# Tensor product of a graph network: rows of the bracket product numbered weight row first

## What is computed

```python
w = _mlp(emb, fc1_w1, fc1_w2)            # relu(emb @ w1) @ w2, per edge: 4 blocks of 16 x 8
s_t = a1 * (einsum('eu,euw->ew', s1, Wss) + einsum('eu,euw->ew', vdot1, Wvv))
v_t = a1 * (einsum('eu,euw->ew', s1, Wsv)[:, :, None] * sh1[:, None, :] + einsum('euk,euw->ewk', v1, Wvs))
w2 = _mlp(emb, fc2_w1, fc2_w2)           # 6 blocks of 8 x 8, used in the same way on s_t and v_t
edge_out = concatenate([tanh(scal), (vecs * tanh(gates)[:, :, None]).reshape(E, 24)], axis=1) * norm[:, None]
return segment_sum(edge_out, edge_dst, num_segments=num_nodes)
```

## Time and profile before

| | us |
|---|---|
| median of three runs | 27219.49 (27213.19 to 27268.23) |
| the profiled execution, span from first to last instruction | 31250.7 |
| of it the tensor product's stretch, 21460 to 31214 | 9754 |
| busy over the span: PE, DVE, POOL, ACT | 15884.3, 15483.3, 15773.3, 5202.4 |

### The profile page before, as it was taken

How to read it: one execution, slowest core, us unless ns; L and a number is a source line. 1 busy time by engine, 2 the same in 40 slices (tenths; PEclk the granted TensorE clock), 3 DMA queues, 4 the chain that set the end, 5 groups by cost and what they waited for, 6 DMA issues and landing times. The chain is left out here.

```text
span 31250.7 us, 456719 instructions
## 1 busy us (share of the span) xinstructions
PE 15884.3 (51%) x102440; PEld 9300.4 (30%) x102441; DVE 15483.3 (50%) x31596; ACT 5202.4 (17%) x13760; POOL 15773.3 (50%) x16798
## 2 busy tenths in 40 slices
PE   7344444445555558973000000035777777777776
PEld 5233333333333338861000000022222222222222
DVE  9444444445555554442111115975555555555556
ACT  4111111111111114431000000001222222222222
POOL 0355555556666664442666666722444444444444
PEclk9555555555555555555555555556777777777777
DMA  2444444432222224521223222212444444444443
GB/s 65 100 121 120 120 120 121 119 91 58 58 59 59 58 56 146 154 81 31 82 81 80 80 80 75 72 47 72 92 93 91 92 92 90 93 91 92 92 92 90
DMA packets 2854618, 2738.27 MB, mean 88 GB/s; under 512 B 1309983, under 2 KB 2216029, under 8 KB 2851618
## 3 DMA queue, kind: packets, MB, share of 16 engines
q1 hardware_dynamic: 2287198, 2308.39, 28.2%
q0 software_dynamic: 412544, 241.53, 5.5%
q10 hardware_dynamic: 153668, 172.93, 2.1%
HBM read 2173.27 MB, written 537.90 MB: 87 GB/s over the span
## 5 line engine op out<-in xcount | busy, mean ns | idle before, releaser
L2219 POOL DMA_INDIRECT rows_x<-x_table,index x3125 | 2973.0, 951 | 4269.0 <-DMA index<-in_src 3504.1
L742 POOL DMA_INDIRECT rows<-split_table,index x3125 | 2985.2, 955 | 3665.8 <-DMA index<-in_src 2695.3
L858 POOL DMA_INDIRECT rows<-x_table,index x3125 | 3296.4, 1055 | 1720.6 <-issue 914.5
L1624 POOL DMA_INDIRECT rows_dram<-rows,place_now x3125 | 3025.4, 968 | 2130.5 <-DVE rows L1552 1145.9
L2333 DVE TENSOR_TENSOR second<-banks,h 128x768 f32<-128x768 f32 x2500 | 1949.2, 820 | 1731.5 <-PE banks L2488 1520.0
L1564 PE MATMUL banks<-row_pieces,hot_turned 128*128 x3125 | 390.1, 289 | 4176.5 <-issue 2856.4
L2325 DVE TENSOR_TENSOR first<-banks,h 128x768 f32<-128x768 f32 x2500 | 1969.4, 820 | 1043.5 <-DMA rows_dram<-rows,place_now 399.2
L1552 DVE TENSOR_REDUCE rows<-banks 128x108 f32<-128x324 f32 x1250 | 490.6, 434 | 4022.9 <-issue 2683.7
L550 PE MATMUL banks<-counts,low_turned 128*128 128x98 f32 x6250 | 1810.5, 438 | 427.2 <-ACT counts L538 318.2
L550 PEld LDWEIGHTS banks<-counts,low_turned 128*128 128x128 f32 x6250 | 1614.6, 317 | 556.0 <-issue 525.0
L2463 PE MATMUL banks<-u_turned,w_tensor 32*128 32x384 f32 (+1 forms) x10000 | 1614.3, 545 | 262.5 <-DVE second L2333 206.0
(11 more groups left out here) (479 smaller groups left out, 34278.3 us busy)
## 6 DMA issues: line engine op xcount, KB each, us to landing
key_row<-dst_rows SPq DMA_DIRECT2D x1250, 320.0 KB
h<-hidden_dram SPq DMA_DIRECT2D x1250, 320.0 KB
acc_moved<-dst_rows SPq DMA_DIRECT2D x625, 320.0 KB
src_row<-in_src_rows SPq DMA_DIRECT2D x625, 320.0 KB
hot_turned<-turned_dram SPq DMA_DIRECT2D x1250, 160.0 KB
hot_dram<-onehot SPq DMA_DIRECT2D x625, 160.0 KB
turned_dram<-hot_turned SPq DMA_DIRECT2D x625, 160.0 KB
a_dram<-a ACTq DMA_DIRECT2D x625, 160.0 KB
```

Source lines behind the costliest of these rows:

```text
L742: nc.gpsimd.indirect_dma_start(out=m["rows"][j][:, t * SPLIT:(t + 1) * SPLIT], out_offset=None, in_=m["split_table"], in_offset=bass.Indir ...
L858: nc.gpsimd.indirect_dma_start(out=m["rows"][j][:, t * C2:t * C2 + F], out_offset=None, in_=m["x_table"], in_offset=bass.IndirectOffsetOnA ...
L1624: nc.gpsimd.indirect_dma_start(out=m["rows_dram"], out_offset=bass.IndirectOffsetOnAxis(ap=m["place_now"][j][:, t:t + 1], axis=0), in_=m[" ...
L2219: nc.gpsimd.indirect_dma_start(out=m["rows_x"][j][:, t * F:(t + 1) * F], out_offset=None, in_=m["x_table"], in_offset=bass.IndirectOffsetO ...
```

## The change

A bracket's row is numbered (k, u), the hidden row first, instead of (u, k). So an `h` tile is loaded with the 16 rows outermost and each repeated eight times. The tables must follow: `w_tensor` is loaded in the old order into a new tile `w_loaded` and permuted by one DVE copy; `w_second`'s 48 small loads go to a new DRAM tensor `second_dram`, from which two loads bring it back in the new order, after a wait for all 48; `unit_sum` and `unit_spread` compare the row number modulo 8 instead of divided by 16.

```diff
@@ stage_directions, SP
-            w, v = m["w_tensor"], m["conv_w1"]
+            w, v = m["w_loaded"], m["conv_w1"]
...
-                    rows = m["w_second"][K16 * u:K16 * (u + 1), 4 * U8 * dotted:4 * U8 * (dotted + 1)]
+                    rows = m["second_dram"][:, u, 4 * U8 * dotted:4 * U8 * (dotted + 1)]
...
-                        sp.dma_start(rows[:, k * U8:(k + 1) * U8], part, allow_slow_non_contiguous=True).then_inc(s["weights"], 16)
+                        sp.dma_start(rows[:, k * U8:(k + 1) * U8], part, allow_slow_non_contiguous=True).then_inc(s["placed"], 16)
...
+            sp.wait_ge(s["placed"], 16 * 6 * U8)
+            for dotted in range(2):
+                here = slice(4 * U8 * dotted, 4 * U8 * dotted + 3 * U8)
+                sp.dma_start(m["w_second"][:, here], m["second_dram"].rearrange("k u c -> (k u) c")[:, here]).then_inc(s["weights"], 16)
@@ stage_directions, DVE
-            for name in ("w_tensor", "w_second"):
+            for name in ("w_loaded", "w_second"):
...
-            dve.wait_ge(s["weights"], 16 * (8 + 6 * U8))
+            dve.wait_ge(s["weights"], 16 * (8 + 2))
+            link(nc.vector.tensor_copy(m["w_tensor"][:, :].rearrange("p (c k u) -> p c k u", k=K16, u=U8),
+                                       m["w_loaded"][:, :].rearrange("p (c u k) -> p c k u", k=K16, u=U8)))
...
-            link(nc.vector.tensor_single_scalar(m["unit_int"][:, :], m["unit_int"][:, :], 4, ALU.arith_shift_right))
+            link(nc.vector.tensor_single_scalar(m["unit_int"][:, :], m["unit_int"][:, :], U8 - 1, ALU.bitwise_and))
@@ sp_group
-                         m["hidden_dram"][bass.ds(g, 1), K16 * k:K16 * (k + 1), :].rearrange("g h e -> (g h) e").unsqueeze(0).broadcast_to([U8, K16, T * P])
+                         m["hidden_dram"][bass.ds(g, 1), K16 * k:K16 * (k + 1), :].rearrange("g h e -> (g h) e").unsqueeze(1).broadcast_to([K16, U8, T * P])
```

More of the change, by code:

```diff
@@ L43 @@
 ONE, FULL = 1, 16
-FROM_ZERO = ("loaded", "x_loaded", "attr_in", "stored", "indexed", "row_in", "pair_in", "a1_in", "emb_in", "weights", "step",
+FROM_ZERO = ("loaded", "x_loaded", "attr_in", "stored", "indexed", "row_in", "pair_in", "a1_in", "emb_in", "weights", "placed", "step",
              "gathered", "moved", "hidden_in", "axes_in", "halves_in", "weights_in", "src_row_in", "marked", "scattered", "own_in", "vec_in", "place_in", "key_in", "key_out", "repeated", "blank_out", "hot_in", "turned_in")
@@ L2058, in _ @@
                 for u in range(U8):
-                    rows = m["w_second"][K16 * u:K16 * (u + 1), 4 * U8 * dotted:4 * U8 * (dotted + 1)]
+                    rows = m["second_dram"][:, u, 4 * U8 * dotted:4 * U8 * (dotted + 1)]
                     for k in range(2):
                         part = m["conv_w2"][:, (1 - k) * P:(2 - k) * P].rearrange("k (o e n) -> k o e n", e=2, n=U8)[:, :, dotted, u]
-                        sp.dma_start(rows[:, k * U8:(k + 1) * U8], part, allow_slow_non_contiguous=True).then_inc(s["weights"], 16)
+                        sp.dma_start(rows[:, k * U8:(k + 1) * U8], part, allow_slow_non_contiguous=True).then_inc(s["placed"], 16)
                     part = m["conv_w2"][:, 256 + 64 * dotted:320 + 64 * dotted].rearrange("k (o n) -> k o n", n=U8)[:, :, u]
-                    sp.dma_start(rows[:, 2 * U8:3 * U8], part, allow_slow_non_contiguous=True).then_inc(s["weights"], 16)
+                    sp.dma_start(rows[:, 2 * U8:3 * U8], part, allow_slow_non_contiguous=True).then_inc(s["placed"], 16)
+            sp.wait_ge(s["placed"], 16 * 6 * U8)
+            for dotted in range(2):
+                here = slice(4 * U8 * dotted, 4 * U8 * dotted + 3 * U8)
+                sp.dma_start(m["w_second"][:, here], m["second_dram"].rearrange("k u c -> (k u) c")[:, here]).then_inc(s["weights"], 16)
             sp.wait_ge(s["permuted"], ONE + 2)
@@ L2720, in build @@
         m["dirs_dram"] = nc.dram_tensor("dirs_dram", (P, COLS * 3), F32, kind="Internal").ap()
+        m["second_dram"] = nc.dram_tensor("second_dram", (K16, U8, 8 * U8), F32, kind="Internal").ap()
         m["dst_rows"] = nc.dram_tensor("dst_rows", (COLS, P), F32, kind="Internal").ap()
@@ L2919, in build @@
                 sb("squared", max(COLS * 3, HALF_WINDOWS * F), into=inner); sb("length", COLS, into=inner)
-                sb("unit_int", P + 1, I32, into=inner); sb("unit", P + 1, into=inner)
-                stage_directions(nc, m, sems("dirs", "halves_in aimed loaded weights stored step cleared permuted to_root rooted"))
+                sb("unit_int", P + 1, I32, into=inner); sb("unit", P + 1, into=inner); sb("w_loaded", 512, into=inner)
+                stage_directions(nc, m, sems("dirs", "halves_in aimed loaded placed weights stored step cleared permuted to_root rooted"))
             with ExitStack() as inner:
```

## The result

The change takes 26539.97 us (median of four runs, 26524.74 to 26628.84) against 27216.34 for the kernel before, run beside it (27169.51 to 27268.23): ratio 0.9764 [0.9749, 0.978], 676 us less. The forecast was 26630, with a range of 26000 to 26930.

What follows compares the result with a forecast made beforehand. The index list, landing behind h in SP's queue, was taken to bound a two-turn loop. 205 x 3.3 = 677 us, less 5 for setup, is 672, scaled to 585 off 27219.49: 26630 us, range 26000 to 26930.

Steps and rivals of the forecast that it cites:

- The engines (8 to 16): Tensor product's h load: with 16 instead of 8 outermost it runs on sixteen DMA engines instead of eight.
- The price of a loop, 3.3 us: Tensor product's two-turn loop: the index list lands earlier, 3.3 us off each loop, bounds 2.0 and 4.8.
- The part from the burst: Transfer of h and hot_half ahead of the list: 6.0 us falls to 4.0 to 2.6, so 2.0 to 3.4 off.
- The part from SP's issue: SP's h issue falls from 621 ns to key_row's 333, so the index list is issued 0.6 us earlier.
- The count, 205 loops: Tensor product: 205 of 312 loops run through the index list, from its 1288 us of the chain.
- The scale, 0.871: The 672 us gain on the profiled span of 31250.7 is scaled by 0.871 to the runs' median: 585 us.
- The setup, 5 us: Stage before the tensor product: w_second's way through DRAM and the new DVE copy cost 5 us, far end 14.
- A mark that was set wrong: Profile after, tensor product: POOL's wait for lists at 4.50 - 3.3 = 1.2 us a turn or little more.
- The split stays: Rival: h's engines don't follow the outer size, so only the setup moves: 27224 us; chance 0.06.
- All loops gain, holes too: Rival: the chain's unnamed holes shrink too, all 312 loops lose up to 4.8 us: 25910; chance 0.17.
- Another wait: Rival: another wait takes the list's place and half the gain is given back: 26925 us; chance 0.10.
- Slower: Rival: one engine reading the same DRAM row eight times running is slow, the burst grows: 27655 us; chance 0.05.

Runs made afterwards that it cites:

- b_early: The kernel before, with each group's index list loaded one group earlier: 25164.38 us, ratio 0.9236.
- a_early: The change, with each group's index list loaded one group earlier: 25160.2 us, ratio 0.9235.
- two_by_rows: The change, with each h load cut into two issues by rows, 8 outermost: 27059.52 us, ratio 0.9945.
- eight_by_cols: The kernel before, with each h load cut into two issues of half the columns, 8 outermost: 27022.91 us, ratio 0.9931.
- two_by_cols: The change, with each h load cut into two issues of half the columns, 16 outermost: 26531.83 us, ratio 0.9754.
- distinct: The change, with each h load reading 128 different rows in plain form from the sixth group on (results not the program's): 26187.4 us, ratio 0.9629.
- one_row: The change, with each h load reading a single DRAM row into all 128 partitions (results not the program's): 26646.1 us, ratio 0.9797.

## Why the prediction was right, and where it was off

**Right: what bounds, and why.** The list behind h on SP's queue, reached from DVE's release and passed on by POOL to PE, is the loop; `b_early` and `a_early` show that the change gains nothing without it. The engines (8 to 16) are what moved it: `two_by_rows` and `eight_by_cols` against `two_by_cols`, and the list's late parts, eight before and none after. Sign and range held.

**The price of a loop, 3.3 us, measured 2.5** (11.34 to 8.82; 2.35 by the chain's pieces). The part from the burst is 2.44 (7.39 to 4.95), inside the 2.0 to 3.4. The part from SP's issue failed: 0.6 was expected because key_row, as many rows of the same size, issues in 333 ns. But 550 ns is what 16 x 8 x 640 takes; only the plain forms of `distinct` and `one_row` come to 333. It gave 0.08 of the list's time.

**The count, 205 loops, was too small.** It came from the shown execution's chain, where the list had 13.2% and unnamed holes over a third; counted, that chain has 191 pieces of the list. The execution that matches the runs has 290, and PE's 295 waits for pieces say the same. 289 x 2.5 = 722 us against 699 measured; by the chain's pieces it is 1935 - 1248 = 687.

**The scale, 0.871, was wrong in kind.** It took 15% off the gain, as if the shown execution were the kernel stretched evenly. It was one long execution, with other shares in its chain, and the stage is 0.904 of what it shows (8815 of 9754), not 0.871. 677 unscaled would have come close, by two errors that cancel: 205 x 3.3 and 289 x 2.5 differ by 45 us. With the scale the forecast was 90 us too high. Why that execution was long was not tried.

**The setup, 5 us, took 21.8,** beyond its stated far end of 14. The price of a load into SBUF (issue 0.43, landing 1.8) was taken for a write to DRAM (0.60 and 10.5, the median landing of the same line after). Its place on the path was right: DVE waits for squared 39.65 us instead of 23.87.

**A mark that was set wrong.** POOL's wait was to fall to 4.50 - 3.3 = 1.2 us a turn. But 3.3 is per loop of two turns. A wait fell from 4.7 us (2818 over 597) to 3.3 (2001 over 601).

**The rivals.** "The split stays" is refuted by the shares. "All loops gain, holes too" had the loops right, 289 of 312, and the holes wrong (1904 and 1913 us). "Another wait" did not show: the stage lost 699 of the 722. "Slower" has its mechanism: repeated reads of a row do cost, as `distinct` against `one_row` shows, but the change stays far from the point at which it would decide. The argument against it, key_row's 208 GB/s at a share of 0.63, was weak: key_row has the same form as `one_row`, which lands late.

**Where the rest of the loop is.** The change shortens PE's hole (4.80 to 2.16 us a wait, above) and does not close it. Windows of after in the loop shown above (PE is the first column after the length, the clock the third from the end):

```profile
22014.00:22015.00 1.00, 0.00 (x0) 0.00 (x0) 0.60 (x1) 0.00 (x0) 0.99 (x2) 1.00 1.14 303
...
22018.00:22019.00 1.00, 1.00 (x8) 0.00 (x0) 0.00 (x0) 0.00 (x0) 0.00 (x0) 0.50 0.06 20
...
22022.00:22023.00 1.00, 1.00 (x7) 0.67 (x9) 0.88 (x5) 0.67 (x2) 0.90 (x1) 0.50 0.12 16
...
22024.00:22025.00 1.00, 0.87 (x11) 0.30 (x4) 1.00 (x2) 0.52 (x3) 0.69 (x2) 1.00 0.02 4
```

and of before:

```profile
22010.00:22011.00 1.00, 0.00 (x0) 0.00 (x0) 0.00 (x0) 0.00 (x0) 0.69 (x2) 1.00 0.65 131
...
22016.00:22017.00 1.00, 1.00 (x8) 0.52 (x8) 0.00 (x0) 0.42 (x1) 0.04 (x1) 0.50 0.00 0
...
22019.00:22020.00 1.00, 1.00 (x15) 0.60 (x11) 1.00 (x6) 0.87 (x2) 0.69 (x2) 1.00 0.08 10
```

PE stands idle while POOL gathers, and the granted clock falls to the lower level (0.50, 1.2 GHz): from 22012 to 22018 before, from 22017 to 22023 after. PE's busy time did not fall with the wait: 6390 and 6425 us, at a mean granted clock of 0.85 and 0.86. In `a_early` PE hardly waits for POOL's pieces:

```profile
PE banks L2534 <- POOL pieces L2236: 8.3, 3, 4.9
```

and the windows of its stretch read:

```profile
18404.00:25115.00 6711.00, 5825.61 (x52495) 2434.82 (x52495) 5534.02 (x11873) 2112.18 (x6249) 4306.45 (x5623) 0.96 0.51 133
```

PE is granted 0.96 on average instead of 0.86, and the same 52495 matmuls take 599 us less. That the clock is part of what the list off the loop earns was read from these rows, not tested by itself.

## What to carry to other kernels

- A list of 2.5 KB that stands behind 800 KB in one queue lands when those have; first ask whether it can be issued ahead (here two lines, 2086 us), then how to make the large loads faster (676 us). With the list ahead, 8 or 16 engines made no difference here (25164 and 25160 us).
- The outermost size of a load set how many DMA engines carried it; here a half share in windows of a microsecond showed it, and which of the sixteen landings of the list were late.
- Before counting on a profile's chain, lay its span beside the runs: here a count from an execution 15% longer was off by 30%, and the factor 0.871 did not mend it.

## What was not expected of the hardware

- Reading one DRAM row 128 times took 4.7 us to land, 128 different rows 3.6 (medians), at the same issue and bytes.
- Half the engines did not take twice as long: a group's h took 5.5 us from the first issue to the last landing on sixteen, 8.2 on eight, 10.5 on four (medians; on four with two issues a tile).
- SP's time for an issue went by the load's form, not its bytes: 333 ns for 128 rows in a plain form, 550 for 16 x 8 rows, 629 for 8 x 16, 617 for 8 x 16 half rows and for 8 x 8 rows, 549 for 4 x 16 rows.
- Small writes to DRAM (16 x 8 floats) landed in 10.5 us (median of 16) where the same into SBUF landed in 1.8.
- Two issues for each tile on eight engines were 0.5% and 0.7% faster than one, though SP issued longer; left open.
